# Mixture shares laid out by DMA through DRAM in place of selection products on TensorE: a two-layer decoder on one NeuronCore

## The reference, cut to what matters

```python
scores = softmax(xt @ Wg.T)                       # T x 16
# the two best of four groups, in them the four best experts
combine = zeros((T, 16)).at[arange(T)[:, None], topi].add(weights)
h = silu(einsum('td,eid->eti', xt, W1)) * einsum('td,eid->eti', xt, W3)   # 16 experts, 176 inner rows each
expert_out = einsum('eti,edi->etd', h, W2)
y = einsum('etd,te->td', expert_out, combine)
z = silu(xt @ Ws1.T) * (xt @ Ws3.T) @ Ws2.T       # shared expert, 352 inner rows
return y + z
```

## Time and profile before

| | |
|---|---|
| median of three runs | 535.25 us (533.11 to 536.31) |
| profiled execution, its own time | 534.2 us |
| its span in the profile | 532.4 us |
| mean granted TensorE clock | 0.987 of full |
| PE busy | 493.6 us (93%), 4694 matmuls |
| DVE busy | 396.9 us (75%) |
| ScalarE busy | 345.2 us (65%) |
| GpSimd busy | 190.4 us (36%) |
| DMA | 21.66 MB, 41 GB/s over the span |

### The profile page before, as it was taken

One profiled execution on the slowest core, in us unless ns is written; L12 is line 12 of the kernel. 1 busy time (PEld: TensorE's weight loads), 2 busy tenths in 40 slices (PEclk: granted clock), 3 DMA queues, 4 the chain that ended last, 5 costly groups with the idle time before them and its releaser, 6 DMA issues.

```text
span 532.4 us, 11834 instructions
## 1 busy us (share of the span) xinstructions
PE 493.6 (93%) x4694; PEld 362.3 (68%) x4721; DVE 396.9 (75%) x917; ACT 345.2 (65%) x601; POOL 190.4 (36%) x288
## 2 busy tenths in 40 slices
PE   5869887899999999999999999999999999999985
PEld 3424533567778788877887878777777676678654
DVE  2787997879677988548996587644876568689984
ACT  5666744766676236894269845588535874976796
POOL 3129986741340150330004072613052221032562
PEclk9987999899999999999999999999999999999999
DMA  8502443220000001000000020200000300000001
GB/s 290 216 0 63 149 162 114 71 81 1 1 3 1 2 10 71 1 2 2 1 1 2 1 80 3 81 1 1 1 1 2 120 1 1 1 2 2 0 27 55
DMA packets 5943, 21.66 MB, mean 41 GB/s; under 512 B 896, under 2 KB 3072, under 8 KB 5120
## 3 DMA queue, kind: packets, MB, share of 16 engines
q1 hardware_dynamic: 5888, 20.91, 11.6%
HBM read 19.86 MB, written 1.05 MB: 39 GB/s over the span
## 4 chain that ended last, share of the span: by engine, by line
PE 67%; DVE 16%; ACT 9%; issue 4%; POOL 3%; DMA 1%; ACTq 0%; DVEq 0%; POOLq 0%
PE ps L1072 24%; PE ps L1106 15%; PE ps L820 4%; DVE nmx L2524 3%; PE ps L951 3%; PE ps L844 2%; PE ps L880 2%; PE ps L1082 2%; PE ps L928 2%; PE ps L875 2%; PE ps L798 2%; PE ps L970 1%; PE ps L931 1%; DVE hl L2642 1%; PE ps L1152 1%
## 5 line engine op out<-in xcount | busy, mean ns | idle before, releaser
L2631 DVE TENSOR_TENSOR hs<-hs,ps 128x512 f32<-128x512 f32 (+1 forms) x68 | 45.2, 668 | 40.0 <-PE ps L1072 27.3
L1952 ACT ACTIVATE hs<-ps 128x512 f32<-128x512 f32 (+1 forms) x68 | 39.4, 581 | 51.1 <-PE ps L1072 42.7
L2524 DVE TENSOR_REDUCE nmx<-ps 128x2 f32<-128x512 f32 (+1 forms) x96 | 60.4, 681 | 7.2 <-PE ps L880 7.1
L556 POOL TENSOR_TENSOR ve<-mv,half 128x2 f32<-128x2 f32 x24 | 7.7, 322 | 149.0 <-DVE mv L2418 149.0
L1106 PE MATMUL ps<-w2h,hh 128*128 128x256 f16 x200 | 54.7, 274 | 0.7 <-DVE hl L2642 0.5
L1106 PE MATMUL ps<-w2h,hl 128*128 128x256 f16 x200 | 54.6, 273 | 0.0
L1106 PE MATMUL ps<-w2l,hh 128*128 128x256 f16 x200 | 54.6, 273 | 0.0
L1959 ACT ACTIVATE hh<-hs 128x512 f16<-128x512 f32 (+1 forms) x52 | 31.5, 611 | 34.5 <-DVE hs L2637 23.3
L2642 DVE TENSOR_TENSOR hl<-hs,hh 128x512 f16<-128x512 f32 (+1 forms) x52 | 40.1, 779 | 8.9 <-ACT hh L1959 8.6
L1911 ACT ACTIVATE pk<-ps 128x512 f32<-128x512 f32 x64 | 34.6, 597 | 12.1 <-PE ps L931 9.6
L1072 PE MATMUL ps<-yah,w1h 128*128 128x256 f16 x200 | 38.4, 274 | 1.9 <-DVE hs L2631 1.9
(11 more groups left out here) (249 smaller groups left out, 1338.5 us busy)
## 6 DMA issues: line engine op xcount, KB each, us to landing
stage<-in_w SPq DMA_DIRECT2D x12, 800.0 KB, 4.3
tstage<-in_tern SPq DMA_DIRECT2D x4, 1024.0 KB, 4.9
cs<-in_ctxT SPq DMA_DIRECT2D x1, 1024.0 KB, 9.4
cd<-in_ctxT SPq DMA_DIRECT2D x1, 1024.0 KB, 4.8
out_x<-xs SPq DMA_DIRECT2D x4, 256.0 KB, 2.2
sels<-in_sel SPq DMA_DIRECT2D x1, 800.0 KB, 9.8
w0s<-in_w SPq DMA_DIRECT2D x1, 768.0 KB, 7.0
xs<-in_x SPq DMA_DIRECT2D x1, 768.0 KB, 8.2
```

What stands on the lines that cost most here:

```text
L1952: act.activation(hs[:, n % 3, 0:w], ps[:, gate_bank(n), 0:w], ACT.Silu).then_inc(e_sil.sem, 1)
L2524: dve.tensor_reduce(nmx[:, int(n % 3 > 0), first + par:first + 2 * heads:2], ps[:, max_bank(it, n) + par, :].rearrange("p (h k) -> p h k", ...
L2631: TT(hs[:, n % 3, 0:w], hs[:, n % 3, 0:w], ps[:, up_bank(n), 0:w], ALU.mult).then_inc(e_hb.sem, 1)
```

## The change

The shares no longer go through TensorE. `ctk` is f32, and `router_experts` writes the 16 shares of a token eight times side by side, so that the (f32) transposes give `cT` with expert p % 16 on partition p. SP writes rows 0 to 15 of `cT` to DRAM (`shares`, 16 KB a batch), waits, and reads them back broadcast to all partitions, two experts at a time (256 KB) into three buffers `shs`. The rows of the weights are permuted on the host so that tiles 0 to 15 hold rows 0 to 127 of experts 0 to 15, tiles 16 to 21 hold the other 48 rows of each expert with expert p % 16 on partition p, and the rest is the shared expert. Pairs 0 to 7 of a batch take their share from `shs`, pairs 8 to 10 from `cT` itself, and pairs 11 and 12 need none. The share product now comes before the up product and reads SBUF alone; `gate`, `inner_high` wait for the up product, `up` for the silu of the pair before. `sels` and its load are gone. The ternary loads now stand among SP's share DMAs. All four lists are in a new order; fillers (`awake`) change from 65 to 81 ahead of gate(0), from 0 to 8 between gate(0) and gate(1), and from 14 to 10 behind the last down product of the mixture.

```diff
+SHARE_PAIRS = E0 // 2
+MASKED_PAIRS = SHARE_PAIRS + (INTER - P) // 8 // 2
+def inner_order():
+    rows = [e * INTER + r for e in range(E0) for r in range(P)]
+    for t in range((INTER - P) // 8):
+        rows += [e * INTER + P + 8 * t + r for r in range(8) for e in range(E0)]
+    return rows + list(range(E0 * INTER, MOE_PAD))
+def share_turn(n):
+    return MASKED_PAIRS * (n // MOE_PAIRS) + min(n % MOE_PAIRS, MASKED_PAIRS)
...
+        shs = sb("shs", [P, 3, 2 * S], F32)
...
-        ctk = sb("ctk", [P, JT, P], F16)
-        cT = sb("cT", [P, T], F16)
+        ctk = sb("ctk", [P, JT, P], F32)
+        cT = sb("cT", [P, 2, S], F32)
...
-            sp.dma_start(sels[:, :], sel0).then_inc(d_sel.sem, 16)
...
-            sp.wait_ge(wst_lo.sem, W_SLICES)
-            for n in range(4):
-                if n:
-                    sp.wait_ge(tern_q.sem, n)
+            def ternary(n):
+                sp.wait_ge(*((tern_q.sem, n) if n else (wst_lo.sem, W_SLICES)))
                 sp.dma_start(tstage[:, :], tern[:, n * TERN:(n + 1) * TERN]).then_inc(d_ts.sem, 16)
+            def shares_out(b):
+                sp.wait_ge(cw_ok.sem, b + 1)
+                sp.dma_start(shares[b].rearrange("(e t) -> e t", e=E0), cT[0:E0, b % 2, :]).then_inc(d_shw.sem, 16)
+                sp.wait_ge(d_shw.sem, 16 * b + 16)
+            def shares_in(b, p):
+                u = SHARE_PAIRS * b + p
+                if u >= 3:
+                    sp.wait_ge(e_hc.sem, share_turn(MOE_PAIRS * ((u - 3) // SHARE_PAIRS) + (u - 3) % SHARE_PAIRS) + 1)
+                sp.dma_start(shs[:, u % 3, :], shares[b:b + 1, 2 * S * p:2 * S * (p + 1)].to_broadcast([P, 2 * S])).then_inc(
+                    d_sh[u % 3].sem, 16)
+            ternary(0)
+            for b in range(B):
+                shares_out(b)
+                for p in range(SHARE_PAIRS):
+                    shares_in(b, p)
+                    if (b, p) in ((1, 3), (2, 7), (3, 3)):
+                        ternary(b)
...
-                    mm = pe.transpose(bank16(0)[:, j * P:(j + 1) * P], ctk[:, j, :], id16[:, :])
+                    mm = pe.transpose(ps[:, 0, j * P:(j + 1) * P], ctk[:, j, :], ident)
...
-                        pe.wait_ge(e_hc.sem, n)
+                        pe.wait_ge(e_sil.sem, n)
...
-            def spread(n):
-                kind, b, p = pair_of(n)
-                if kind == "hash":
-                    return
-                pe.wait_ge(e_sil.sem, n + 1)
-                for par in range(tiles_of(n)):
-                    mm = pe.matmul(ps[:, gate_bank(n), par * S:(par + 1) * S],
-                                   sels[:, (2 * p + par) * P:(2 * p + par + 1) * P],
-                                   cT[:, b * S:(b + 1) * S], start=True, stop=True)
-                mm.then_inc(e_c.sem, 1)
...
-                act.activation(cT[:, b * S:(b + 1) * S], bank16(0)[:, 0:S], ACT.Copy).then_inc(cw_ok.sem, 1)
+                if b >= 2:
+                    act.wait_ge(e_hc.sem, MASKED_PAIRS * (b - 1))
+                act.activation(cT[:, b % 2, :], ps[:, 0, 0:S], ACT.Copy).then_inc(cw_ok.sem, 1)
...
-                act.wait_ge(e_hc.sem, n + 1)
+                act.wait_ge(e_hb.sem, n + 1)
...
-                link(TT(cw[:, :, :], mk[:, :, 0:E0], mr[:, :, 0:E0], ALU.subtract))
-                link(dve.tensor_copy(ctk[:, :, 0:E0], cw[:, :, :]))
-                TT(ctk[:, :, E0:2 * E0], cw[:, :, :], ctk[:, :, 0:E0], ALU.subtract).then_inc(ctk_ok.sem, 1)
+                if b:
+                    dve.wait_ge(cw_T.sem, b)
+                for j in range(JT):
+                    last = TT(ctk[:, j, :].rearrange("p (r e) -> p r e", e=E0), mk[:, j, None, 0:E0].to_broadcast([P, 8, E0]),
+                              mr[:, j, None, 0:E0].to_broadcast([P, 8, E0]), ALU.subtract)
+                last.then_inc(ctk_ok.sem, 1)
...
             def times_up(n):
-                dve.wait_ge(e_sil.sem, n + 1)
                 if n < ALL_MOE:
                     dve.wait_ge(e_b.sem, n + 1)
+                if n < ALL_MOE and n % MOE_PAIRS < MASKED_PAIRS:
+                    dve.wait_ge(e_hc.sem, share_turn(n) + 1)
+                else:
+                    dve.wait_ge(e_sil.sem, n + 1)
                 w = tiles_of(n) * S
                 TT(hs[:, n % 3, 0:w], hs[:, n % 3, 0:w], ps[:, up_bank(n), 0:w], ALU.mult).then_inc(e_hb.sem, 1)
             def times_share(n):
-                dve.wait_ge(e_hb.sem, n + 1)
-                dve.wait_ge(e_c.sem, n + 1)
-                w = tiles_of(n) * S
-                TT(hs[:, n % 3, 0:w], hs[:, n % 3, 0:w], ps[:, gate_bank(n), 0:w], ALU.mult).then_inc(e_hc.sem, 1)
+                kind, b, p = pair_of(n)
+                if kind == "hash" or p >= MASKED_PAIRS:
+                    return
+                dve.wait_ge(e_sil.sem, n + 1)
+                mine = hs[:, n % 3, :].rearrange("p (k t) -> p k t", k=2)
+                if p < SHARE_PAIRS:
+                    u = SHARE_PAIRS * b + p
+                    dve.wait_ge(d_sh[u % 3].sem, 16 * (u // 3) + 16)
+                    share = shs[:, u % 3, :].rearrange("p (k t) -> p k t", k=2)
+                else:
+                    dve.wait_ge(cw_ok.sem, b + 1)
+                    share = cT[:, b % 2, None, :].to_broadcast([P, 2, S])
+                TT(mine, mine, share, ALU.mult).then_inc(e_hc.sem, 1)
...
             project(1, 0)
+            awake(3, 14)
             maxima_turned(0)
+            awake(1, 1)
...
             pe.wait_ge(mx_ok.sem, 33)
             gate(0)
-            pe.wait_ge(mx_ok.sem, 34)
+            router_turned(1)
+            maxima_turned(2)
+            first_output(1)
+            scores_exp(2, 0)
             up(0)
-            router_turned(1)
-            first_output(1)
-            pe.wait_ge(cw_ok.sem, 1)
-            spread(0)
+            awake(0, 4)
+            scores_exp(2, 1)
+            awake(0, 4)
+            scores_exp(2, 2)
             gate(1)
-            maxima_turned(2)
             up(1)
-            scores_exp(2, 0)
-            spread(1)
+            scores_exp(2, 3)
```

More of the change, by code:

```diff
@@ L376, in decoder @@
         d_wst = [sig(f"d_wst{n}", 16) for n in range(STAGES)]
+        d_sh = [sig(f"d_sh{n}", 16) for n in range(3)]
+        d_shw = sig("d_shw", 16)
         d_ts = sig("d_ts", 16)
@@ L1455, in _ @@
-            spread(19)
-            project(4, 1)
             logits(2)
-            gate(20)
             up(20)
             values(3, 0)
+            gate(20)
+            scores_exp(3, 3)
+            down(17)
+            down(18)
             values(3, 1)
+            stack(4, 0)
             scores_exp(3, 4)
-            stack(4, 0)
-            spread(20)
+            stack(4, 1)
+            gate(21)
+            stack(4, 2)
+            up(21)
+            up(22)
             back(3, 0)
-            down(18)
@@ L1546, in _ @@
[L1546 to L1560 removed]
+            values(4, 0)
+            gate(33)
+            scores_exp(4, 4)
+            values(4, 1)
+            down(31)
+            scores_exp(4, 5)
@@ L1561, in _ @@
+            stack(5, 1)
+            stack(5, 2)
+            up(33)
+            up(34)
+            gate(34)
+            down(32)
+            scores_max(5, 0)
+            down(33)
+            back(4, 0)
+            scores_max(5, 1)
+            stack(5, 3)
             gate(35)
@@ L1712, in _ @@
             scores_max(7, 5)
+            gate(58)
+            gate(59)
+            tail_turned(6)
+            maxima_turned(7)
             down(57)
-            gate(59)
-            maxima_turned(7)
-            tail_turned(6)
             scores_exp(7, 0)
+            scores_exp(7, 1)
             down(58)
-            scores_exp(7, 1)
             down(59)
@@ L2862, in _ @@
-            first_low(3)
+            context_factors(1)
+            times_up(2)
+            context_added(1)
+            moments_of('router', 1)
+            times_share(3)
+            times_up(3)
+            first_low(3)
+            times_share(4)
+            times_up(4)
+            inner_low(2)
+            queries_keys(3, 0)
             experts_lo('moe', 1, 0)
             times_share(5)
-            queries_keys(3, 0)
+            inner_low(3)
+            times_up(5)
+            queries_keys(3, 1)
```

1141 lines of the change are left out of this document (519 added, 622 removed).

## The result

The changed kernel took 539.34 us in the median of 8 runs (537.15 to 542.4), against 535.04 for 8 runs of the kernel before: a ratio of 1.0084, 95% interval 1.0058 to 1.0110. It is **slower by 4.5 us**; I had forecast 525.2, and said 515 to 537. An execution that ran slower than its kernel's others at a lower granted clock counts in a median but not in a ratio; there is one each in e4, e14 and e15. The profiled execution took 540.2 us, with a span of 538.7.

What follows compares the result with a forecast made beforehand. TensorE, busy 288.5 of 293.8 us in the mixture, was taken as the bound. Terms -10.9, +0.4, +2.5 and -2, the rest 0, summed to -10.0: 525.2 us against the 535.25 median, range 515 to 537.

Steps and rivals of the forecast that it cites:

- Selection products gone: Mixture, TensorE's queue: 50 pairs of selection matmuls at 0.22 us leave, all inside the bound stage, -10.9 us.
- rival B: Mixture: peaks of DVE and ScalarE take half of the 10.9 us, so 530 us; chance 0.11.
- DVE's share products: Mixture, DVE: 52 products become 44 with SBUF operands; a 4.8 us surplus from meeting GpSimd; priced at 0.
- cover: Mixture: TensorE's 288 us hide DVE's share products, as DVE stays at three quarters of the stage; without it +4.8 us.
- rival C: Mixture: whole GpSimd instructions block 12 of 44 share products, 20 us of DVE, 530 us; sign: mean over 1 us; chance 0.06.
- Waits within a pair: Mixture pairs: up waits only for the silu, but the next gate can be 0.69 us later; 0, ends -4 and +3.7.
- that loss doubled: Mixture pairs: upper end, +3.7 us, for gates waiting on the up product, which had lost 3.7 us so far.
- rival D: Mixture: share product inside the gate-to-gate loop, half exposed, 15.2 us, 540 us; sign: gate waits of 10 us; chance 0.11.
- Mixture 0 behind two DMAs: Start of mixture 0: shares' write and read put gate(1) at 124.8 instead of 119.52; +2.5 us, ends 0 and +5.3.
- mixtures 1 to 3: Starts of later batches: chain needs 5.9 us, old gap 4.3 in batch 3, new lists copy earlier; 0, up to +3.
- New lists in the head: Head: filled hole avoids the low clock, against 16 more fillers; -2 us, ends -4.3 and +3.5.
- Later than 115: Head: sign of being wrong, gate(0) starting later than 115 us because of the head's fillers.

Runs made afterwards that it cites:

- e4: Changed kernel with its broadcast reads taken from an input in DRAM, without the write of the shares and its wait: 537.24 us, ratio 1.0038.
- e14: Changed kernel with the up product ahead of the share product and the shares read early from an input: 534.53 us, ratio 1.0007.
- e15: Changed kernel with 100 matmuls of 128x256 put ahead of the up groups and overwritten by them: 543.29 us, ratio 1.0150.
- e5: Kernel before with its 100 selection products left out and nothing else changed, share product still reading PSUM: 527.74 us, ratio 0.9895.
- e9: e5 with only the share product's second operand moved from PSUM to a constant tile in SBUF: 534.81 us, ratio 1.0008.
- e1: Kernel before without selection products, share product reading a constant SBUF tile, up waiting for the silu alone: 533.14 us, ratio 0.9987.
- e8: Changed kernel with the up product first and the share product behind it, next gate waiting for up alone: 535.58 us, ratio 1.0036.
- e13: e4 with one wait more: up also waits for the share product of the pair before; operand stays in SBUF: 544.31 us, ratio 1.0171.
- e10: e4 with the share product's operand in PSUM for 32 pairs, and up also waiting for the earlier share product: 541.21 us, ratio 1.0126.
- e11: Changed kernel's functions in the lists of the kernel before, reading an input in place of the shares, no write: 539.57 us, ratio 1.0097.
- e2: Changed kernel's functions, with shares by DMA and share product ahead of up, in the lists of the kernel before: 554.65 us, ratio 1.0358.
- e3: Changed kernel with the old lists up to gate(0) on all four engines, the new ones behind: 538.82 us, ratio 1.0085.
- e17: e9 with GpSimd's causal masks and first two ternary weight passes cut to a few columns: 524.24 us, ratio 0.9813.
- e16: e5 with GpSimd's causal masks and first two ternary weight passes cut to a few columns: 523.76 us, ratio 0.9812.

## Why the prediction was wrong, point by point

The way from the kernel before to the changed one, in ratios: products out 0.9895 (e5), operand to SBUF 1.0008 (e9), up's wait loosened 0.9987 (e1), new lists and functions with the old order in the pair and no round trip 1.0007 (e14), round trip 1.0036 (e8), share product first 1.0084. The steps: -5.6, +6.0, -1.1, +1.1, +1.5, +2.6 us. The first two are resolved, and so are the last one and the last two taken together; the middle two and the round trip by itself are within their intervals. They are the steps of this way, not prices that hold in any order: the first two were taken in the old lists. Against the sum of the forecast, -10.0, the kernel came out 14.5 us worse. Of these, 5.3 are the selection products, 6.0 the operand, 2.6 the order in the pair, and the other 0.6 is what the unresolved steps leave.

**Selection products gone, -10.9: the step that failed first**, in the sentence "what leaves TensorE's queue inside the mixture is worth its full stream time, unless another engine is just behind". (The sum is slightly off as well: 50 pairs of 0.22 us are 11.0.) It measured -5.6 in the kernel before, and put back into the changed one 3.5, net of the clock. DVE and ScalarE were just behind, and not only in the two peaks of the earlier trace rows: with the products gone they hold 40% of the chain, and taking the share products away as well gave 3.4 us more. Which waits ended last, pair by pair, was not followed. This is rival B's mechanism, half comes back. I read PE's 288.5 of 293.8 us as a bound; the 5.3 us of idle time say only that there was little room, not that all else could run ahead.

**DVE's share products, 0, with +4.8 without cover: mis-sized.** The surplus itself was right: 4.8 forecast, 3.7 by the groups of the changed kernel ((728 - 683) x 32 + (873 - 683) x 12 ns, 683 being the product from PSUM). The cover was not there: 5.5 us of it cost 6.0 in e9. This was rival C: whole GpSimd passes block the product, and they block it inside the loop that TensorE waits for. Its size was too high, 20 us of DVE for 12 meetings where e9 had nine and 5.5 us, and its sign, a mean over 1 us, never came: 728 ns. C got 0.06 because hl lives with the same meeting; but hl was paying too. In the new lists the price is smaller, 2.4 us by e13 against e10, and not resolved, so that the operand cost the changed kernel itself 6 us is not shown.

**Waits within a pair, 0 between -4 and +3.7.** The looser wait (-4) gave 1.1 us in the old lists, within its interval. The order was bounded as "that loss doubled", 3.7 us; the gates' loss for DVE's hs went from 3.7 to 8.1 us, and turning the order round gave 2.6 us of the time. It is rival D's mechanism at a sixth of its price; that the rest is hidden, as I had argued with 3.4 us of loop in 5.3 of pair, fits this and was not tested. Its sign, 10 us of such waits, was set too high as well. In the old lists e11 against e1 gives 5.9 us, with other changes in it.

**Mixture 0 behind two DMAs, +2.5.** Near in size, and partly by luck, since the term was a middle between 0 and 5.3: the round trips of all batches cost 2.5 us (e4), or 1.5 (e8 against e14). The second gate group came 7.5 us after the end of the copy cT, where I had said some 7. That **mixtures 1 to 3** pay 0 holds for the new lists, whose share products have no DMA among their releasers; that it is the lists which hide it is shown by e2 and e11.

**New lists in the head, -2.** The low clock near 40 us went, as forecast, but three stretches of 3.4 us at 1.2 GHz stand elsewhere in the head, at 53.3, 84.0 and 111.3 us, against the 10.2 and 3.5 us of the earlier trace rows. The first of them:

```profile
53.30:56.70 3.40, 3.40 (x30) 2.23 (x31) 3.33 (x6) 1.03 (x2) 3.40 (x3) 0.50 0.00 0
```

e3 puts the worth of the new head at 0.0, with 2 us either way, so -2 is at the edge of what it allows. The first gate group starts at 116.93. "Later than 115" was among my signs of being wrong, but it was a poor one: the kernel before starts it at 115.2.

**What I did not count: the clock.** The kernel before had no stretch at 1.2 GHz in the mixture. The changed one has two of 3.4 us, at 343.4 and 398.0. The timeline ahead of the first, and the clock in two windows:

```profile
338.62 1.98 POOL L640 TENSOR_SCALAR tstage<-tstage,winv 128x2048 f32<-128x2048 f32 x1
339.89 1.24 DVE L2616 TENSOR_TENSOR hs<-hs,shs 128x512 f32<-128x512 f32 x1 [1.84 <-ACT hs L1918]
340.69 2.20 POOL L642 TENSOR_SCALAR tstage<-tstage 128x2048 f32<-128x2048 f32 x1
341.06 2.10 DVE L2621 TENSOR_TENSOR hl<-hs,hh 128x256 f16<-128x256 f32 x1
...
343.22 0.28 PE L1122 MATMUL ps<-w2h,hh 128*128 128x256 f16 x1 [2.02 <-DVE hl L2621]
```

```profile
340.00:343.40 3.40, 1.38 (x13) 1.00 (x12) 3.40 (x3) 0.98 (x2) 3.22 (x3) 1.00 0.00 0
343.40:346.80 3.40, 3.40 (x18) 2.32 (x16) 3.24 (x9) 0.63 (x1) 1.52 (x1) 0.50 0.29 55
```

A share product of 0.69 us takes 1.24, and a low part of half size 2.10 in place of 0.42, each beside a pass of GpSimd; the down group waits 2.02 us for it; TensorE is busy 1.38 of 3.4 us; and for the next 3.4 it runs at half its clock, at most 1.7 us of work lost. That the clock fell because of the wait is argued from this order of events. No run takes away this one meeting. e8 and e14 have no such stretch in the mixture (their clock rows are 9 in every slice there), which can be part of what turning the order round gives. The mean granted clock over the runs behind the ratios was 0.985 for the changed kernel, 0.989 in e8 and 0.991 in e14: by the difference times the span at most 2.1 of the 2.6 us and 3.3 of the 4.1, by my estimate. The bound is a wide one, since e3 took the changed kernel's time at 0.980. How much is the clock and how much the waits is not told apart.

## What to carry to other kernels

An engine at 98% of a stage is a bound for work that is added, not a price for work that is taken away: take the work out by itself, with nothing in its place, before building what replaces it (here 5.6 of 10.9 us came back, and in the same lists the operand of the replacement cost 6.0). A DVE product whose second operand is in PSUM took 0.69 us at most beside all of GpSimd's passes here (e5), and moving the operand to SBUF puts whole GpSimd passes into the loop it stands in (e9). Lists written for one set of waits can't be read as evidence on another: the same wait cost nothing that could be told in one order and 7.1 us in the other.

## What the runs showed that I had not expected

- The collision is whole or nothing: a product either keeps its time or stands until the GpSimd instruction ends. 39 of 48 SBUF products of e9 ran at 0.68 to 0.69 us and nine took 0.81 to 2.15 us, for 5.5 us in all; without the wide GpSimd passes the longest was 1.19.
- GpSimd seems to pay as well: its busy time over the whole span was 196.2 us in e9 and 192.4 in e5, with the same instructions, and 162.0 in e17 against 159.3 in e16. It was 190.4 in the kernel before, so some 2 us of such differences come without the operand.
- Cutting those passes alone, with the operand in PSUM (e16 against e5), gave 0.83%, 4.4 us, though GpSimd is busy under 30% of the mixture; hl's mean fell from 778 to 686 ns, 4.4 us of DVE. The masks also end sooner for what waits for them, so what gave the 4.4 us was not separated.
- A write of 16 KB to DRAM was ready for the read 1.46 us after its issue, sooner than the 2.2 us that I had taken from a write of 256 KB.
